# Four layer normalisations: the scaling of each tile moved from VectorE to ScalarE

## What is computed

```python
def _layernorm(x, axis=-1, eps=1e-05):
    m = jnp.mean(x, axis=axis, keepdims=True)
    v = jnp.var(x, axis=axis, keepdims=True)
    return (x - m) / jnp.sqrt(v + eps)

x = x + jnp.tanh(g_xattn[0]) * _L0_xattn_ref(_layernorm(x), ctx_1024, W, b)
x = x + jnp.tanh(g_ffn[0]) * _L0_ffn_ref(_layernorm(x), w_up, w_down)
x = x + jnp.tanh(g_xattn[1]) * _L1_xattn_ref(_layernorm(x), ctx_1024, mask, Wq, ..., 16)
x = x + jnp.tanh(g_ffn[1]) * _L1_ffn_ref(_layernorm(x), gate_w, up_w, down_w, s_in, s_in_down)
```

## Time and profile before

| what | value |
|---|---|
| median of 3 runs | 1818.28 us (1814.18 to 1821.37) |
| the profiled execution, its own time | 1823.66 us |
| its span in the trace | 1821.9 us |
| VectorE busy | 1421.6 us, 78% of the span, 2437 instructions |
| TensorE busy (products) | 1371.2 us, 75%, 8120 instructions |
| ScalarE busy | 692.5 us, 38%, 2105 instructions |
| GpSimd busy | 243.9 us, 13%, 197 instructions |
| TensorE's granted clock, mean | 0.89 of full speed |

### The profile page before, as it was taken

How to read it: one execution, slowest core, us unless ns; L and a number is a source line. 1 busy time by engine, 2 the same in 40 slices (tenths; PEclk the granted TensorE clock), 3 DMA queues, 4 the chain that set the end, 5 groups by cost and what they waited for, 6 DMA issues and landing times.

```text
span 1821.9 us, 24307 instructions
## 1 busy us (share of the span) xinstructions
PE 1371.2 (75%) x8120; PEld 705.4 (39%) x8120; DVE 1421.6 (78%) x2437; ACT 692.5 (38%) x2105; POOL 243.9 (13%) x197
## 2 busy tenths in 40 slices
PE   5044737799787978698778978797869886988663
PEld 4021315344453436344543345343634453434321
DVE  6988896878787687787787878768777778786695
ACT  2112206451455227441644146422734164425310
POOL 1102200131003200230013100320013001310000
PEclk9556868899889989999999989998999999999888
DMA  9175761042101420233004210142023300420012
GB/s 348 68 243 146 188 143 36 6 88 64 42 1 35 93 59 14 35 62 77 25 7 87 58 48 1 35 93 59 14 35 65 75 24 6 87 58 24 7 24 51
DMA packets 267433, 120.08 MB, mean 66 GB/s; under 512 B 244090, under 2 KB 244602, under 8 KB 265750
## 3 DMA queue, kind: packets, MB, share of 16 engines
q1 hardware_dynamic: 267286, 118.27, 26.5%
HBM read 49.04 MB, written 8.39 MB: 32 GB/s over the span
## 4 chain that ended last, share of the span: by engine, by line
issue 43%; DVE 26%; PE 18%; DMA 4%; SPq 4%; ACT 3%; POOL 2%; POOLq 0%; DVEq 0%; ACTq 0%
PE bank L1075 13%; PE bank L1164 5%; DVE amax L826 2%; DVE pair L835 2%; DVE hid L831 2%; SPq L314 2%; DVE th L868 2%; SPq L303 1%; DVE pair L850 1%; DMA region<-region 1%; ACT region L535 1%; DVE pair L843 1%; DMA hqt<-pair 1%; DVE sc L797 1%; DVE stats L686 1%
## 5 line engine op out<-in xcount | busy, mean ns | idle before, releaser
L1164 PE MATMUL bank<-w_dn,region 128*128 128x512 fp8e4 x1024 | 243.7, 386 | 40.0 <-DMA region<-region 40.0
L1075 PE MATMUL bank<-w_up,xt 128*128 128x512 fp8e4 x1024 | 248.6, 391 | 32.7 <-ACT region L499 17.4
L1075 PE MATMUL bank<-w_gate,xqt 128*128 128x512 bf16 x512 | 147.9, 416 | 122.2 <-DVE th L868 78.4
L508 ACT ACTIVATE th<-bank,half_cg 128x512 f32<-128x512 f32 x128 | 88.0, 687 | 350.2 <-PE bank L1075 350.2
L426 POOL TENSOR_TENSOR region<-g,region 128x512 f16<-128x512 f32 x128 | 178.9, 1402 | 300.9 <-ACT region L499 292.9
L868 DVE SCALAR_TENSOR_TENSOR th<-th,bank 128x512 f32<-128x512 f32 x128 | 87.6, 684 | 138.4 <-ACT th L508 138.3
L535 ACT ACTIVATE region<-bank,nm 128x77 f32<-128x77 f32 x512 | 160.0, 345 | 68.2 <-DVE nm L914 68.2
L1075 PE MATMUL bank<-w_down,hqt 128*128 128x512 bf16 x512 | 134.3, 422 | 56.9 <-DMA hqt<-pair 56.9
L496 ACT ACTIVATE g<-bank 128x512 f32<-128x512 f32 x128 | 76.4, 597 | 247.2 <-PE bank L1075 188.2
L1164 PEld LDWEIGHTS bank<-w_dn,region 128*128 128x128 f16 x1024 | 101.0, 99 | 167.4 <-issue 52.0
L1075 PEld LDWEIGHTS bank<-w_up,xt 128*128 128x128 f16 x1024 | 102.0, 101 | 163.5 <-issue 55.4
(11 more groups left out here) (206 smaller groups left out, 2473.6 us busy)
## 6 DMA issues: line engine op xcount, KB each, us to landing
xin<-in_x SPq DMA_DIRECT2D x16, 512.0 KB, 4.1
out_x<-x SPq DMA_DIRECT2D x16, 512.0 KB, 3.0
region<-in_w_up_t SPq DMA_DIRECT2D x1, 4096.0 KB, 12.9
hid<-in_gate_w SPq DMA_DIRECT2D x4, 1024.0 KB, 5.2
x<-in_gate_w SPq DMA_DIRECT2D x4, 1024.0 KB, 6.1
hid<-in_up_w SPq DMA_DIRECT2D x4, 1024.0 KB, 5.2
x<-in_up_w SPq DMA_DIRECT2D x4, 1024.0 KB, 5.8
hid<-in_down_w SPq DMA_DIRECT2D x4, 1024.0 KB, 4.9
```

What stands on the lines that cost most here:

```text
L508: eng.activation(th[:, u % 2, :], bank[4][:, :], ACT.Tanh, scale=half_cg[:, :]).then_inc(sg["th"], 1)
L1075: last = mm(out, lhs, rhs, start=(n == 0), stop=(n == len(pairs) - 1))
L1164: last = mm(bank[2 + t % 2][:, :], ht[i][:, t % 2, f, :], w_dn[:, f, :], start=(f == 0 and i == 0), stop=(f == KF - 1 and i == 1))
```

## The change

VectorE no longer makes the normalised tiles. It computes one small tile, shift = -mean x scale, of one value per token, and ScalarE makes each normalised tile by one activation of the function Identity: scale x input + shift, both read per token. This is done for all four normalisations. New counters shift1 to shift4 tell ScalarE that the shifts are there, and x4n tells VectorE that the tiles of the fourth normalisation are; the rounding waits for it. ScalarE's four (or two) activations stand in its list at the step or slot at which VectorE's stood. For the second one this is ahead of ScalarE's part of attend of the same step, for the tiles 0 and 1 of the fourth behind it, for tiles 2 and 3 behind the up projection's slot 1, for the third ahead of the Tanh of its slot, and for the first at the end of phase_b, behind the queries. The core of the diff:

```diff
@@ -206,7 +207,7 @@
                  "loaded_o loaded_up loaded_dn loaded_piece0 loaded_piece1 split wout_hi wout_lo ctx_psum ctx_done tern_part tern_done wsum_all "
                  "wmax_part wmax_all pe_passed dve_passed piece_read piece_codes wt_done sp_passed tanh_done").split()
         per = dict(xin=32, var1=1, var2=1, var3=1, var4=2, rstd1=1, rstd2=1, rstd3=1, rstd4=2,
-                   xn1=4, xn2=4, xn3=4, tr1=4, tr2=4, tr3=4, xh1=4, xh2=4, xh3=4, xl1=4, xl2=4, xl3=4,
+                   shift1=1, shift2=1, shift3=1, shift4=2, x4n=4, xn1=4, xn2=4, xn3=4, tr1=4, tr2=4, tr3=4, xh1=4, xh2=4, xh3=4, xl1=4, xl2=4, xl3=4,
                    sc1=4, nm1=4, ex1=4, p1t=4, p1h=4, p1l=4, o1=4, x1=4,
                    up=16, g32=16, hh=16, hl=16, sq=16, ms=2, rms=2, ht_even=64, ht_odd=64, dn=4, x2=4,
                    qp=4, q32=4, qh=4, ql=4, sc3=16, nm3=16, p3=16, p3t=16, p3h=16,
@@ -468,6 +469,21 @@
             act.wait_ge(sm["tern_part"], 2)
             eng.activation(dump, stage_w, ACT.Abs, accum_out=wsum[:, 0:1]).then_inc(sm["tern_part"], 1)
 
+            def norm(stage, g, src):
+
+                want(act, f"shift{stage}", g)
+                scale = rn if stage == 2 else rstd[:, 0]
+                for t in range(TILES):
+                    eng.activation(xn[:, t, :], src[:, t, :], ACT.Identity, bias=shift[:, 0, t:t + 1],
+                                   scale=scale[:, t:t + 1]).then_inc(sg[f"xn{stage}"], 1)
+
+            def x4(g, a):
+
+                want(act, "shift4", g, a + 1)
+                for t in (2 * a, 2 * a + 1):
+                    eng.activation(xb[:, t, :], x3[:, t, :], ACT.Identity, bias=shift[:, 1, t:t + 1],
+                                   scale=rstd[:, 1, t:t + 1]).then_inc(sg["x4n"], 1)
+
             def x_hi(stage, g, t):
                 want(act, f"tr{stage}", g, t + 1)
                 eng.activation(xt[0][:, :, t * P:(t + 1) * P],
@@ -485,6 +501,8 @@
                 if (u := tile1_at(n, 4)) is not None:
                     want(act, "p1t", g, u + 1)
                     eng.activation(pt1[0][:, u % 2, :], bank[u % 2][0:M, P:2 * P], ACT.Copy).then_inc(sg["p1h"], 1)
+                if n == NORM2_AT:
+                    norm(2, g, xin)
                 for t in T2_AT.get(n - 1, ()):
                     x_hi(2, g, t)
 
@@ -542,6 +560,8 @@
                         want(act, "out3", g, t)
                     eng.activation(ot[0], bank[3][:, :].rearrange("p (k t) -> p k t", k=KD),
                                    ACT.Copy).then_inc(sg["oth"], 1)
+                if n == min(X4_STEPS):
+                    x4(g, 0)
 
             def phase_a(g3, g1):
                 for n in range(STEPS):
@@ -562,15 +588,17 @@
                     if s4 is not None and s in GU_AT:
                         tanh4(s4, GU_AT[s])
 
+            norm(1, 0, xin)
             phase_a(None, 0)
-            phase_b(0, None)
+            phase_b(0, None, 1)
             with act.Fori(0, GROUPS - 2) as g:
                 phase_a(g, g + 1)
-                phase_b(g + 1, g)
+                phase_b(g + 1, g, g + 2)
             g = GROUPS - 1
             phase_a(g - 1, g)
-            phase_b(g, g - 1)
+            phase_b(g, g - 1, None)
             phase_a(g, None)
+            x4(g, 1)
             for u in range(4 * TILES):
                 tanh4(g, u)
 
@@ -699,7 +727,7 @@
                     settle()
                 eng.tensor_scalar(dst, mv[:, s, ts, 1], LN_EPS, None, ALU.add).then_inc(sg[f"var{stage}"], 1)
 
-            def norm(stage, g, src):
+            def norm(stage, g):
 
                 want(dve, f"rstd{stage}", g)
                 scale = rstd[:, 0, :]
@@ -714,9 +742,8 @@
                     done(eng.tensor_tensor(rn[:, :], rn[:, :], scale, ALU.mult))
                     settle()
                     scale = rn[:, :]
-                for t in range(TILES):
-                    eng.tensor_scalar(xn[:, t, :], src[:, t, :], mv[:, 0, t, 0:1], scale[:, t:t + 1],
-                                      ALU.subtract, ALU.mult).then_inc(sg[f"xn{stage}"], 1)
+                eng.scalar_tensor_tensor(shift[:, 0, :], mv[:, 0, :, 0], -1.0, scale, ALU.mult,
+                                         ALU.mult).then_inc(sg[f"shift{stage}"], 1)
 
             def x_lo(stage, g, t):
                 want(dve, f"xh{stage}", g, t + 1)
@@ -852,13 +879,13 @@
             def x4(g, a):
 
                 want(dve, "rstd4", g, a + 1)
-                for t in (2 * a, 2 * a + 1):
-                    done(eng.tensor_scalar(xb[:, t, :], x3[:, t, :], mv[:, 1, t, 0:1], rstd[:, 1, t:t + 1],
-                                           ALU.subtract, ALU.mult))
-                settle()
+                ts = slice(2 * a, 2 * a + 2)
+                eng.scalar_tensor_tensor(shift[:, 1, ts], mv[:, 1, ts, 0], -1.0, rstd[:, 1, ts], ALU.mult,
+                                         ALU.mult).then_inc(sg["shift4"], 1)
 
             def quant_x4(g, a, parts):
                 src = xb[:, 2 * a:2 * a + 2, :].rearrange("p t d -> p (t d)")
+                want(dve, "x4n", g, 2 * a + 2)
                 quantise(src, x_sc[:, :], x_g[:, :], parts, sg["xq"], tiles=(2 * a, 2 * a + 1))
 
             def hidden(g, u, buf=hid):
```

More of the change, by code:

```diff
@@ L78 @@
 WT_DONE = WT_AT[-1]
-DVE_STEPS = 141
+DVE_STEPS = 137
 RADD = bass.bass_isa.ReduceOp.add
@@ L162, in build @@
                for i in range(2)]
+        shift = sb("shift", [P, 2, TILES], F32)
         stats = sb("stats", [P, 2, TILES, 6], F32)
@@ L551, in phase_a, with phase_b @@
                         attend(g3, n)
-            def phase_b(g, s4):
+            def phase_b(g, s4, g1):
                 for s in range(SLOTS):
@@ L556, in phase_b @@
                         up(g, s)
+                    if s4 is not None and s == min(X4_AT):
+                        x4(s4, 1)
+                    if s == SLOT_NORM3:
+                        norm(3, g, xb)
+                    if s == SLOT_Q + NC and g1 is not None:
+                        norm(1, g1, xin)
                     if s == SLOT_T3:
@@ L731, in norm1 @@
                 norm_stats(1, g)
-                norm(1, g, xin)
+                norm(1, g)
             def stage1(g, n):
@@ L757, in stage1 @@
                 if n == NORM2_AT:
-                    norm(2, g, xin)
+                    norm(2, g)
                 for t in T2_AT.get(n - 1, ()):
@@ L969, in phase_b @@
                     if s == SLOT_NORM3:
-                        norm(3, g, xb)
+                        norm(3, g)
                     if s == SLOT_T3:
```

## The result

The changed kernel takes **1883.66 us** (median of 4 runs), the kernel before 1817.03 us (median of its 4 runs). The ratio is **1.0363, 95% interval 1.034 to 1.0385**. The direction was as forecast; the size, +66.6 us against +42, was not, and 1883.66 lies above the range of 1838 to 1880 us.

A forecast was written before the change was run, and what follows sets the result against it. Turns between engines were taken as the bound: 5.3 us a group, 37.1 over seven, start -1.4, last group +1.2, gives +36.9; with 5.1 for the clock, +42 us on the median 1818.28, forecast 1860 us, range 1838 to 1880.

The forecast's parts named there:

- What bounds the kernel, and the direction: Whole kernel: turns between engines set the end, not one full engine; slower by over 0.5% given chance 0.90.
- The rival with VectorE as the bound: ScalarE's tiles are ready before VectorE and TensorE want them: 7.1 us won per group, 1768 us; chance 0.05.
- the one that evens out: Rival: later waits have slack, delays under 1.3 us a group, between -9 and +9 us, 1818 us; chance 0.05.
- Price of an activation: ScalarE's new 128x512 activations: 0.81 us each, one every 0.70 us in a row.
- cheap activations: Rival: activations cost as with one operand and the shift isn't held up: +20 us, 1838 us; chance 0.2.
- Second, third, and fourth normalisation of tiles 0 and 1: Attention and feed-forward stages: work waits behind ScalarE's new activations, +1.8, +1.9 and +1.5 us a group.
- Fourth, tiles 2 and 3: Fourth normalisation's second pair: the shift waits some 1.2 us for GpSimd, then ScalarE's pair; +0.1 us a group.
- First normalisation: Next group's first normalisation, beside TensorE's wait and products: taking it from VectorE gains nothing, 0 us.
- first, start, end and the rest: First normalisation, the kernel's first and last stretches and the remainder, taken together: -0.2 us.
- The clock: Output projection behind the second normalisation: two more groups at TensorE's lower clock, 2 x 2.54 = 5.1 us.
- The rival in which the clock goes down everywhere: TensorE's lower clock at all the places counted: 37 + 22 = 59 us, 1877 us; chance 0.15.
- From the sum to the forecast: Whole kernel: profiled execution's own sum 1865.7 us, put at 1860 us because that execution lay 5.4 above the median.

The follow-up runs named there:

- e11: Kernel before the change, only the second normalisation moved to ScalarE, placed behind ScalarE's own copy of that step: 1818.31 us, ratio 0.9989.
- e8: Changed kernel, ScalarE's activations of the second and third normalisation placed behind its own copy and Tanh of the same step: 1858.92 us, ratio 1.0202.
- e4: Kernel before the change, only the first normalisation moved to ScalarE: 1821.83 us, ratio 1.0002.
- e3: Kernel before the change, only the fourth normalisation (both pairs of tiles) moved to ScalarE: 1852.3 us, ratio 1.0178.
- e1: Kernel before the change, only the second normalisation moved to ScalarE, ahead of ScalarE's own copy: 1844.71 us, ratio 1.014.
- e5: Changed kernel, unread extra TensorE products in pauses at the second and third normalisation and before a group's first gate product: 1873.32 us.
- e13: Changed kernel, unread extra TensorE products only before the first and second gate product of a group: 1875.69 us, ratio 1.0284.
- e14: Changed kernel, unread extra TensorE products only at the second normalisation, third up-projection and third normalisation: 1873.96 us, ratio 1.0291.
- e6: Kernel before the change, unread extra TensorE products at the second and third normalisation and before a group's first gate product: 1834.68 us, ratio 1.0058.
- e15: Kernel before the change, second normalisation on ScalarE behind its own copy, plus unread extra TensorE products in all the pauses: 1806.45 us, ratio 0.9918.
- e10: Kernel before the change, unread extra TensorE products at second and third normalisation, first and second gate product and third up-projection: 1815.7 us, ratio 0.9981.
- e7: Kernel before the change, VectorE making the second and third normalisation twice, ScalarE untouched: 1863.63 us, ratio 1.0224.

## Why the prediction was wrong, step by step

- **What bounds the kernel, and the direction: right.** Turns between engines, not VectorE's 78%. The rival with VectorE as the bound and the one that evens out are both refuted: VectorE lost 55 us of work and the span grew by 59.6.
- **Price of an activation: right.** 803 ns and one each 0.71 us (0.81 and 0.70 forecast), which leaves nothing of cheap activations.
- **Second, third, and fourth normalisation of tiles 0 and 1: the waits right.** 1.81, 1.9 and 1.5 us in groups without a low stretch, 1.8, 1.9 and 1.5 forecast. e11 shows the cause of the first. For the third, e8 shows that the Tanh behind the activations isn't the only thing awaited: without it in their way the 1.9 us stay.
- **Fourth, tiles 2 and 3: the step right, its surroundings missed.** The shift is held up as forecast (1.10 us, 1.2 forecast), but the pair also holds back a Gelu, GpSimd's next instruction comes later, and L815 pays 0.7 us for it. Forecast 0.1, measured 0.76: 4.6 us over seven groups that the sum has not.
- **First normalisation: right.** e4 has +1.5 us with an interval around nothing. But first, start, end and the rest together are -5.6 us where -0.2 was forecast, most of it 0.64 us a group in n1 to n2, which e4 alone doesn't have (46.52 us). Why isn't shown, and it hides as much of the miss.
- **The clock: this is the step that failed.** The term was 5.1 us: two more groups with a slow projection, and nothing anywhere else. The spans of the profiled executions differ by 59.6 us where the sum has 42.0. Filling pauses takes 25 to 28 of the 66.6 us back, and low stretches are left, so the clock has about that or more. The term was too small at three places. The projection is slow in all seven groups, where three had it before: four more, not two (4.01 to 4.41 us instead of 2.76), and n4a to n4b is 7.0 us over its term. Behind tiles 2 and 3, where I gave the clock no price, n4b to m1 is 17.6 us over its term, of which L815 is 4.6. Behind the third normalisation, where I had a bound of 6 us but put nothing into the sum, n3 to n1 is 3.4 us over. Behind tiles 2 and 3 the pause had not even grown, and why the clock falls late in it isn't shown.
- **The rival in which the clock goes down everywhere** (1877 us, chance 0.15) was nearest. Its sum of 59 us is what the spans differ by, but that is partly luck: it had no price for the products behind tiles 2 and 3 either, nor for L815, and it put more on the other two places than they measured. From the sum to 1877 it lost the 5.4 us of the next point.
- **From the sum to the forecast: 5 us more.** I took 5.4 us off, the distance of the profiled execution of the kernel before from its median. The changed kernel's profiled execution (1883.62 us) stands at its median, so that the distance wasn't a property of both.

Open: why a given group has a low stretch at the projection. e4 and e3 have it in five and in six of seven groups, the kernel before in three, with the same work ahead of it in the pass.

## What to carry to other kernels

When work goes to an engine that is less busy, cost the instruction that then stands behind it in that engine's list, not the engine's share: the same four activations cost 24 us ahead of a copy and nothing behind it (e1, e11). A delay on a chain that TensorE waits for can cost more than itself, here 66.6 us for 38.7, because products come out of the pause at half the clock; price it in every group and at every place where TensorE has just waited, also where the pause didn't grow. Filling some of TensorE's pauses can move the low stretch onto products without slack: it won 8 to 10 us of the 29 in the changed kernel (e5, e13, e14) and lost 13 in the kernel before (e6). With all five places filled, a reorder that alone gave nothing is worth 1.6 us a group (e15, 193.8 us, e10, 195.4).

## What I had not expected of the hardware

- Filling four of TensorE's pauses, among them one of 5.4 us, made the kernel before 13 us slower (e6, 1834.68 us beside 1821.79): the low stretch moved from 948 to 955 us, where two products with slack lay, to one later pause, and the products behind that had none.
- A delay made by VectorE (e7), 30 us by its own rows, costs 41.8 us (33 to 49 by the interval).
- A VectorE instruction of 128x64, L815, takes 0.96 us instead of 0.25 beside GpSimd's L427, and L845 1.26 instead of 0.43 beside L426 in four of seven groups of the kernel before. So a GpSimd instruction that starts later can cost 0.7 us without any of VectorE's having changed.
